# Block 1 of a gated linear-attention kernel: three pair sums on GpSimd, five transposed rows in place of eight on TensorE, and new call orders on all engines

## Chip, cores and metric

The kernel runs on one core of one Trainium2 chip. The metric is the device time of the launch in microseconds (us); for the kernel before it is the median of three runs. Five engines have queues of their own: TensorE (PE), VectorE (DVE), ScalarE (ACT), GpSimd (POOL) and SyncE (SP), which here issues nearly all DMAs. PEld is TensorE's weight load.

## The reference, cut to what matters

The input is 8 sequences of 1024 tokens of width 128. First comes a gated recurrence in 16 heads of size 8, then a feed-forward part of width 512 with three layers between. Both are followed by a residual sum and a normalisation.

```
q, k, v, fg = x@Wq, x@Wk, x@Wv, sigmoid(x@Wf + bf)      # each (b, s, 16, 8)
state = state * fg[..., None] + v[..., None] * k[..., None, :]   # 8x8 per head, step by step
out   = einsum('bhij,bhj->bhi', state, q)
out   = layernorm(out)*gamma + beta;  out = out*silu(x@Wg);  x = layernorm(x + out@Wout)
h = silu(x@w1.T*s1) * (x@w2.T*s2); h = gelu(h@h1.T*..); h = gelu(h@h2.T*..); x = layernorm(x + h@w3.T*..)
```

The sum over j in the einsum is what the change touches: for each block the kernel has eight rows (j = 0 to 7) of Q times state, and they have to be added.

## The kernel before

The 8192 tokens are cut into 16 blocks of 512. Channels lie on the 128 partitions, tokens along the row. `KJ` and `QJ` hold for one block the eight rows of k (then of the state) and of q (then of q times state), 128x512 each, in two buffers that alternate. For blocks 1 to 15 k and q are computed (`project_k`, `project_q`), copied to `qk` by ACT (`copy_k`, `copy_q`), written to memory (`send(n, 1)` for k, `send(n, 0)` for q) and read back spread over the partitions in halves of four rows and 1024 KB (`fetch(n, which, half)`, which = 1 for k).

For a block n the order of the attention part is: `kv` (DVE, two rows each) and `kv_gp` (POOL) multiply k by v; `scan` (DVE, 8 of them) runs the recurrence along the tokens; `qs` (DVE, four, two rows each) multiplies by q; the eight rows are summed; `sum_transposed` (PE) transposes the result into the PSUM bank `back`; `stats_o` (DVE), `rstd_of(n, "o")` (POOL) and `norm_o` (ACT) normalise; `transpose_y`, `affine`, `gated_y` (POOL), `attention_out` (PE), `residual_1`, `stats_1`, `rstd_of(n, "1")`, `norm_1`, `transpose_x1`, `x1_hi` and `x1_lo` follow. The feed-forward part is split into high and low parts of the left operand: `up_hi`/`up_lo(n, t)`, `silu`, `hmul`, then for layers 1 and 2 `mid_open`, `mid_hi`, `mid_lo` with the low parts made by `lo` on POOL, and `last_begin`/`last_rest`. A feed-forward product of 128x512 is one matmul; a projection is two matmul records.

The eight rows are summed in three ways. In block 0 PE adds all eight by transposing into the same bank (`sum_j`). In blocks 2 to 15 DVE adds three times (`add`), POOL once (`add_gp`, line 544), and PE transposes the one row that is left, 4 transposes of 128x128. Block 1 is in `EARLY` (line 27): nobody adds, and PE sums all eight rows by transposes that accumulate, 8 for each of 4 chunks, 32 in all (line 2310). POOL makes four of its k times v rows (`kv_gp(1, 4)` to `(1, 7)`).

Every engine's order is written out by hand as a list of calls; the waits are semaphores inside the helpers. An engine runs its list strictly in order, SP too, so a call that waits holds back all calls behind it. The PSUM bank `front` is shared by all projections other than v, and a table (`FREED`) says which reader each use waits for. `keep_busy` on PE is filler that computes nothing. Everything from block 0's first `up_hi` on is in `rest()`, entered after `set_flag`.

Of the kernel before, what the change touches and what calls it, by code (L numbers as in the profile page):

```python
# [3 lines left out]
def build_program(nc, x_d, xT_d, wproj_d, wffn_d, w3_d, w3s_d, cols_d, ident_d, out_d):  # L4
# [10 lines left out]
    P, T, HD = 128, 512, 8  # L15
# [8 lines left out]
    NPAIR = HD // 2  # L24
    ADDS = 3

    EARLY = range(1, 2)
    XB, XTB, GB = 4, 4, 3
# [9 lines left out]
    with ctx:  # L38
# [86 lines left out]
        def adds_gpsimd(n):  # L125
            return sum(m not in EARLY for m in range(1, n))

# [120 lines left out]
        def _(e):  # L248
# [72 lines left out]
            load_projections(1)  # L321
            load_cols()
            load_xT(1)
            load_weights(0)
            load_weights(1)
            load_weights(2)
            load_xT(2)
            send(1, 1)
# [5 lines left out]
            load_weights(3)  # L334
            send(2, 1)
            load_x(0)
            fetch(1, 0, 0)
# [7 lines left out]
            send(3, 0)  # L345
            load_x(1)
            fetch(2, 0, 1)
            fetch(3, 1, 0)
            send(4, 1)
            fetch(3, 1, 1)  # L350
            load_x(2)
            load_xT(5)
            load_x(3)
            send(4, 0)
            fetch(3, 0, 0)
            load_x(4)
            load_xT(6)
            fetch(3, 0, 1)
            fetch(4, 1, 0)
            fetch(4, 1, 1)  # L360
            fetch(4, 0, 0)
            load_xT(7)
            fetch(4, 0, 1)
            load_xT(8)
            load_x(5)
            send(5, 1)
            fetch(5, 1, 0)
            store(0)
            fetch(5, 1, 1)
            send(5, 0)  # L370
            load_x(6)
            load_xT(9)
            load_x(7)
            store(1)
            fetch(5, 0, 0)
            send(6, 1)
            fetch(5, 0, 1)
            fetch(6, 1, 0)
            send(6, 0)
            fetch(6, 1, 1)  # L380
            store(2)
            fetch(6, 0, 0)
            send(7, 1)
            fetch(6, 0, 1)
            load_xT(10)
            send(7, 0)
            fetch(7, 1, 0)
            fetch(7, 1, 1)
            send(8, 1)
            fetch(7, 0, 0)  # L390
            fetch(7, 0, 1)
            load_x(8)
            store(3)
            fetch(8, 1, 0)
            fetch(8, 1, 1)
            load_x(9)
            send(8, 0)
            send(9, 1)
            fetch(8, 0, 0)
            load_xT(11)  # L400
            fetch(8, 0, 1)
            load_x(10)
            fetch(9, 1, 0)
            send(9, 0)
            load_xT(12)
            fetch(9, 1, 1)
            store(4)
            fetch(9, 0, 0)
# [3 lines left out]
            store(5)  # L412
            send(10, 1)
            fetch(10, 1, 0)
            load_x(11)
            fetch(10, 0, 0)
            fetch(10, 1, 1)
            load_x(12)
            fetch(10, 0, 1)
            send(11, 1)  # L420
            send(11, 0)
            fetch(11, 1, 0)
            fetch(11, 1, 1)
            fetch(11, 0, 0)
            store(6)
            load_x(13)
            send(12, 1)
            fetch(12, 1, 0)
            fetch(11, 0, 1)
            send(12, 0)  # L430
            fetch(12, 1, 1)
            store(7)
            fetch(12, 0, 0)
            load_xT(14)
            send(13, 1)
            fetch(12, 0, 1)
            fetch(13, 1, 0)
            fetch(13, 1, 1)
            load_x(14)
            send(13, 0)  # L440
            store(8)
            load_xT(15)
            fetch(13, 0, 0)
            send(14, 1)
            fetch(14, 1, 0)
            fetch(13, 0, 1)
            store(9)
            fetch(14, 1, 1)
            send(14, 0)
# [4 lines left out]
            fetch(15, 1, 0)  # L454
            fetch(15, 1, 1)
            store(11)
# [3 lines left out]
            load_x(15)  # L460
# [12 lines left out]
        def _(e):  # L473
# [2770 lines left out]
```

## Time and profile before

| quantity | value |
|---|---|
| time, median of 3 runs | 511.95 us (511.7 to 512.26) |
| time of the profiled execution | 511.54 us |
| its span | 509.6 us |
| granted TensorE clock, mean | 0.997 of full |
| PE busy | 496.3 us, 97% |
| DVE busy | 448.7 us, 88% |
| ACT busy | 406.4 us, 80% |
| POOL busy | 311.7 us, 61% |
| DMA traffic | 87.33 MB, mean 171 GB/s |

The busy time of an engine is the union of its records. Matmul records overlap, since their ends are modelled, so the spacing from one group's start to the next is the real cost of matmuls, and a small gap can hide beneath the tail of a record. A row of the timeline merges like instructions: its second number is the stretch covered by all of them. The bracket at a row's end is idle time of that engine ahead of it, with the releaser.

### The profile page before, as it was taken

The numbers are of one execution on the slowest core, as the hardware profiler recorded it, in microseconds if no ns is written. First come the engines' busy times: TensorE is split into PE (matmuls) and PEld (weight loads), VectorE is DVE, ScalarE is ACT, GpSimd is POOL, SyncE is SP. The second block draws the span as 40 slices with busy tenths as digits, with TensorE's granted clock in tenths as the row PEclk, the third lists the DMA queues.
The fourth block names the chain that finished last, engine by engine and source line by source line (L and its number), as shares of the span: only waits on it lengthen the run. The fifth ranks groups of instructions, "written<-read, shape, count | busy, mean of one in ns | idle before, by whom it ended". The sixth has DMA issues, their size and how long they took to land.

```text
span 509.6 us, 7946 instructions
## 1 busy us (share of the span) xinstructions
PE 496.3 (97%) x2528; PEld 382.4 (75%) x2528; DVE 448.7 (88%) x708; ACT 406.4 (80%) x839; POOL 311.7 (61%) x363
## 2 busy tenths in 40 slices
PE   8999999999999999999999999999999999999995
PEld 5576777777878777786877777786877777787995
DVE  4999989999999899998999999899999999993352
ACT  5775968888887888978797788988778987868863
POOL 0751848668392766848385765938477683929432
PEclk9999999999999999999999999999999999999998
DMA  6899999953994497689969675799719483710001
GB/s 244 205 267 236 255 263 241 230 125 84 275 221 104 104 246 177 154 195 249 259 183 234 142 185 125 186 222 244 196 51 235 130 194 94 183 25 1 23 23 44
DMA packets 21500, 87.33 MB, mean 171 GB/s; under 512 B 2512, under 2 KB 3280, under 8 KB 13520
## 3 DMA queue, kind: packets, MB, share of 16 engines
q1 hardware_dynamic: 21168, 86.46, 67.9%
q8 instruction: 22, 0.36, 0.3%
q10 hardware_dynamic: 288, 0.33, 0.2%
q14 instruction: 22, 0.18, 0.1%
HBM read 74.72 MB, written 12.06 MB: 170 GB/s over the span
## 4 chain that ended last, share of the span: by engine, by line
PE 48%; POOL 17%; DVE 13%; issue 13%; ACT 7%; DMA 1%; POOLq 0%; DVEq 0%; ACTq 0%
PE F L2342 26%; POOL h1lo L479 5%; PE front L2243 5%; POOL h2lo L479 5%; PE back L2441 4%; DVE KJ L1590 3%; DVE QJ L1597 2%; POOL KJ L541 2%; DVE QJ L1605 2%; PE ps_v L2243 2%; PE back L2328 2%; PE back L2227 1%; DMA out<-res 1%; POOL rstd_o L511 1%; POOL y L553 1%
## 5 line engine op out<-in xcount | busy, mean ns | idle before, releaser
L903 ACT ACTIVATE h<-F,cols 128x512 f32<-128x512 f32 x120 | 80.7, 686 | 17.0 <-PE F L2342 16.5
L479 POOL TENSOR_TENSOR h1lo<-h,h1hi 128x512 fp32r<-128x512 f32 x60 | 76.5, 1291 | 12.8 <-ACT h1hi L896 12.7
L547 POOL TENSOR_TENSOR QJ<-QJ 128x512 f32<-128x512 f32 x14 | 18.0, 1284 | 108.0 <-DVE QJ L1605 108.0
L479 POOL TENSOR_TENSOR h2lo<-h,h2hi 128x512 fp32r<-128x512 f32 x60 | 77.2, 1309 | 4.9 <-ACT h2hi L896 4.7
L1590 DVE TENSOR_TENSOR_SCAN KJ<-g,carry,KJ 128x512 f32<-128x512 f32 x64 | 78.5, 1263 | 0.9 <-ACT carry L829 0.8
L1590 DVE TENSOR_TENSOR_SCAN KJ<-g,KJ 128x512 f32<-128x512 f32 x64 | 74.3, 1202 | 1.6 <-POOL KJ L528 0.7
L1597 DVE TENSOR_TENSOR QJ<-QJ,KJ 128x1024 f32<-128x1024 f32 x60 | 72.9, 1237 | 0.2
L2342 PE MATMUL F<-h2hi,whi 128*128 128x512 f32 (+1 forms) x256 | 71.6, 415 | 0.8 <-ACT h L903 0.7
L2342 PE MATMUL F<-h1hi,whi 128*128 128x512 f32 (+1 forms) x256 | 68.9, 410 | 1.6 <-DVE h L1654 1.3
L2342 PE MATMUL F<-h1lo,whi 128*128 128x512 f32 (+1 forms) x256 | 67.4, 400 | 0.2 <-POOL h1lo L479 0.2
L2342 PE MATMUL F<-h2lo,whi 128*128 128x512 f32 (+1 forms) x256 | 65.7, 397 | 0.0
L2243 PE MATMUL front<-xT,wproj 128*128 128x512 f32 x122 | 62.9, 597 | 1.4 <-ACT gate L843 0.9
L2342 PEld LDWEIGHTS F<-h1hi,whi 128*128 128x128 f32 x256 | 44.9, 188 | 22.3 <-issue 9.4
L2342 PEld LDWEIGHTS F<-h2hi,whi 128*128 128x128 f32 x256 | 46.6, 188 | 18.6 <-issue 5.7
L2441 PEld LDWEIGHTS back<-w,h 128*128 128x128 f32 x480 | 57.9, 191 | 2.7 <-issue 0.2
L2441 PE MATMUL back<-w,h 128*128 128x128 f32 x480 | 58.4, 275 | 0.0
L2342 PEld LDWEIGHTS F<-h1lo,whi 128*128 128x128 f32 x256 | 45.9, 188 | 12.2 <-issue 2.4
L2342 PEld LDWEIGHTS F<-h2lo,whi 128*128 128x128 f32 x256 | 46.1, 188 | 11.0 <-issue 1.4
L1574 DVE TENSOR_TENSOR KJ<-ps_v,KJ 128x1024 f32<-128x1024 f32 x44 | 52.6, 1206 | 0.0
L1605 DVE TENSOR_TENSOR QJ<-QJ 128x1024 f32<-128x1024 f32 x42 | 51.2, 1220 | 1.4
L890 ACT ACTIVATE h<-F,cols 128x512 f32<-128x512 f32 x60 | 40.3, 685 | 14.7 <-PE F L2342 14.1
L541 POOL TENSOR_TENSOR KJ<-KJ,v_sb 128x512 f32<-128x512 f32 x32 | 41.0, 1288 | 13.0 <-ACT v_sb L864 8.8
(184 smaller groups left out, 935.9 us busy)
## 6 DMA issues: line engine op xcount, KB each, us to landing
KJ<-qk_bounce SPq DMA_DIRECT2D x30, 1024.0 KB, 9.9
QJ<-qk_bounce SPq DMA_DIRECT2D x30, 1024.0 KB, 11.0
qk_bounce<-qk SPq DMA_DIRECT2D x30, 256.0 KB, 4.6
x_in<-in_x SPq DMA_DIRECT2D x16, 256.0 KB, 11.4
xT<-in_xT SPq DMA_DIRECT2D x15, 256.0 KB, 11.5
out<-res SPq DMA_DIRECT2D x15, 256.0 KB, 3.3
wraw<-in_wffn SPq DMA_DIRECT2D x2, 1024.0 KB, 6.6
wraw<-in_wffn SPq DMA_DIRECT2D x2, 256.0 KB, 4.6
```

Source lines behind the costliest of these rows:

```text
L479: e.tensor_tensor(h_lo[layer][:, t, :w], h[:, t, :w], h_hi[layer][:, t, :w].bitcast(f32), ALU.subtract).then_inc(lo_done[layer], 1)
L541: e.tensor_tensor(K, K, v_sb[:, :WIDTH[n]], ALU.mult).then_inc(kv_gp_done, 1)
L547: e.tensor_tensor(first, first, other, ALU.add).then_inc(add_gp_done, 1)
L890: e.activation(h[:, t, :WIDTH[n]], F[2 * (t % 2)][:, :WIDTH[n]], ACT.Silu, scale=S1[t]).then_inc(silu_done, 1)
L903: e.activation(dst[:, t, :WIDTH[n]], F[t][:, :WIDTH[n]], ACT.Gelu, scale=scale[t]).then_inc(gelu_done[layer], 1)
L1574: e.tensor_tensor(K, vb, K, ALU.mult).then_inc(kv_done, 1)
L1590: e.tensor_tensor_scan(K, g[:, :WIDTH[n]], K, init, ALU.mult, ALU.add).then_inc(scan_done, 1)
L1597: e.tensor_tensor(Q, Q, rows(KJ, n)[:, 2 * p:2 * p + 2, :], ALU.mult).then_inc(qs_done, 1)
L1605: e.tensor_tensor(first, first, other, ALU.add).then_inc(add_done, 1)
L2243: return e.matmul(bank[:, :WIDTH[n]], weights, xT[n % XTB][:, :WIDTH[n]], start=True, stop=True)
L2342: return e.matmul(out, whi[:, cs], part, start=start, stop=stop)
L2441: return e.matmul(back[:, chunk(c)], h3[:, k, chunk(c)], w3[:, k, :], start=k == 0, stop=k == NH - 1)
```

## The change

`EARLY_PAIRS = 3` is new. In block 1 POOL now adds rows 0+1, 2+3 and 4+5 of `QJ` in place (`add_pair(1, 0)` to `(1, 2)`), each after the `qs` that makes the pair. PE then transposes rows 0, 2, 4, 6 and 7: 5 for each of 4 chunks, 20 in place of 32. `sum_transposed(1)` waits for the three adds besides the four `qs`.

```diff
+    EARLY_PAIRS = 3
-            return sum(m not in EARLY for m in range(1, n))
+            return sum(EARLY_PAIRS if m in EARLY else 1 for m in range(1, n))
+            def add_pair(n, p):
+                e.wait_ge(qs_done, NPAIR * (n - 1) + p + 1)
+                first, other = (rows(QJ, n)[:, k, :] for k in (2 * p, 2 * p + 1))
+                e.tensor_tensor(first, first, other, ALU.add).then_inc(add_gp_done, 1)
                 if n in EARLY:
                     e.wait_ge(qs_done, NPAIR * n)
-                else:
-                    e.wait_ge(add_gp_done, adds_gpsimd(n + 1))
-                terms = HD if n in EARLY else 1
+                e.wait_ge(add_gp_done, adds_gpsimd(n + 1))
+                terms = [*range(0, 2 * EARLY_PAIRS, 2), *range(2 * EARLY_PAIRS, HD)] if n in EARLY else [0]
```

The rest of the diff, some 2400 lines, reorders calls. No other call is added or dropped on any engine, only their places change, in nearly every block by a few positions. The moves that the prediction speaks of:

```diff
+            load_xT(4)
+            send(3, 1)
+            send(2, 0)
             fetch(2, 1, 0)
-            load_xT(4)
-            send(2, 0)
             fetch(2, 1, 1)
-            send(3, 1)
...
             rstd_of(0, "1")
+            add_pair(1, 0)
             lo(1, 0, 0)
+            add_pair(1, 1)
+            add_pair(1, 2)
             lo(1, 0, 1)
             lo(1, 0, 2)
+            lo(1, 0, 3)
             rstd_of(1, "o")
-            lo(1, 0, 3)
```

- SP (first part of the diff above): the first half of block 2's k is fetched only behind `send(3, 1)` and `send(2, 0)`.
- DVE, old order: `scan(1,6)`, `half_norm("1")`, `qs(1,0)`, `qs(1,1)`, `set_flag`, `x1_lo(0)`, `scan(1,7)`, `qs(1,2)`, `hmul(0,0)`, `hmul(0,1)`, `qs(1,3)`, `hmul(0,2)`, `kv(2,0)`, `hmul(0,3)`, `scan(2,0)`, `stats_o(1)`. New order: `half_norm("1")`, `qs(1,0)`, `set_flag`, `x1_lo(0)`, `qs(1,1)`, `qs(1,2)`, `hmul(0,0)`, `hmul(0,1)`, `scan(1,6)`, `scan(1,7)`, `hmul(0,2)`, `hmul(0,3)`, `qs(1,3)`, `kv(2,0)`, `scan(2,0)`, `stats_o(1)`.
- PE ahead of `rest()`: `project_v(2)` moves from behind `transpose_x1(0)` to behind `sum_j(7)`; `count_low_parts` moves from ahead of `project_k(3)` to behind `transpose_x1(0)`.
- PE in `rest()`, old order: `up_hi(0,0)`, `up_hi(0,1)`, `up_lo(0,0)`, `up_lo(0,1)`, `project_q(3)`, the up products of t = 2 and t = 3, `sum_transposed(1)`, `mid_open(1,0,0..3)`, `mid_hi(1,0,1..3)`, `mid_lo(1,0,0)`. New order: `up_hi(0,0)`, `up_lo(0,0)`, `up_hi(0,1)`, `up_lo(0,1)`, t = 2, `project_q(3)`, t = 3, `project_k(4)`, `mid_open(1,0,0..3)`, `mid_hi(1,0,1)`, `sum_transposed(1)`, `mid_hi(1,0,2..3)`, `mid_lo(1,0,0)`.
- PE, block 4: `up_lo(4,2)` moves from ahead of `up_hi(4,3)` to behind `sum_transposed(5)`, so that `up_lo(4,3)` and `project_gate(6)` alone stand between it and `mid_open(1,4,0)`.
- PE, block 9: `last_rest(8)` moves ahead of `up_hi(9,1)`. Block 14: `project_gate(15)` moves from between `up_lo(14,3)` and `mid_open(1,14,0)` to between `mid_lo(1,13,3)` and `mid_open(2,13,2)`.
- PE, the end: `last_half(0)` moves from behind `tail_lo_products(2,1,3)` to ahead of `tail_lo_products(2,1,0)`, so that `last_half(1)` follows the last low products at once.

## Rows read from the trace of the kernel before

**Rows 1.** The page: busy us, share and instructions; granted clock; DMA share, 40 slices.

```profile
PE 496.3 (97%) x2528; PEld 382.4 (75%) x2528; DVE 448.7 (88%) x708; ACT 406.4 (80%) x839; POOL 311.7 (61%) x363
...
PEclk9999999999999999999999999999999999999998
DMA  6899999953994497689969675799719483710001
```

**Rows 2.** The page: shares by engine of the chain that ended last.

```profile
PE 48%; POOL 17%; DVE 13%; issue 13%; ACT 7%; DMA 1%; POOLq 0%; DVEq 0%; ACTq 0%
```

**Rows 3.** Timeline of PE, 41 to 53 us: start, length, work [idle before <-releaser].

```profile
41.44 0.60 PE L2227 MATMUL back<-ident,x 128*128 128x128 f32 x4
41.88 1.02 PE L2243 MATMUL ps_v<-xT,wproj 128*128 128x512 f32 x2
42.74 1.02 PE L2243 MATMUL front<-xT,wproj 128*128 128x512 f32 x2
43.99 1.19 PE L2342 MATMUL F<-x1hi,whi 128*128 128x512 f32 x4 [0.23 <-issue]
...
47.21 0.73 PE L2342 MATMUL F<-x1hi,whi 128*128 128x512 f32 x2 [0.24 <-DVE h L1654]
...
49.17 3.65 PE L2310 MATMUL back<-ident,QJ 128*128 128x128 f32 x32
52.58 3.98 PE L2342 MATMUL F<-h1hi,whi 128*128 128x512 f32 x16
```

**Rows 4.** Timeline of DVE, 42 to 73 us.

```profile
42.77 0.68 DVE L1649 TENSOR_TENSOR x1lo<-back,x1hi 128x512 fp32r<-128x512 f32 x1
...
49.83 1.21 DVE L1574 TENSOR_TENSOR KJ<-ps_v,KJ 128x1024 f32<-128x1024 f32 x1
...
51.79 1.22 DVE L1590 TENSOR_TENSOR_SCAN KJ<-g,KJ 128x512 f32<-128x512 f32 x1
...
72.90 0.69 DVE L1649 TENSOR_TENSOR x1lo<-back,x1hi 128x512 fp32r<-128x512 f32 x1 [2.24 <-ACT x1hi L883]
```

**Rows 5.** Timeline of POOL, 49 to 57 us.

```profile
49.73 3.78 POOL L479 TENSOR_TENSOR h1lo<-h,h1hi 128x512 fp32r<-128x512 f32 x3 [10.38 <-ACT h1hi L896]
...
55.83 1.31 POOL L479 TENSOR_TENSOR h1lo<-h,h1hi 128x512 fp32r<-128x512 f32 x1
```

**Rows 6.** Timeline of ACT, then of SP, around 44 and 34 us.

```profile
43.80 0.60 ACT L819 ACTIVATE qk<-front 128x512 f32<-128x512 f32 x1 [1.07 <-PE front L2243]
...
33.71 0.51 SPq L294 DMA_DIRECT2D KJ<-qk_bounce  x1
```

**Rows 7.** KJ's fetches, us from issue to landing: at 33.71; all 30; at 13.8.

```profile
DMA to landing us min/median/max: 15.3/15.3/15.3
...
DMA to landing us min/median/max: 7.7/9.9/21.9
...
KJ<-qk_bounce SPq DMA_DIRECT2D x1, 1024.0 KB, 12.4
```

**Rows 8.** Timeline of PE at four later waits.

```profile
71.39 0.66 PE L2227 MATMUL back<-ident,x 128*128 128x128 f32 x4 [0.45 <-ACT x L848]
...
314.71 0.63 PE L2310 MATMUL back<-ident,QJ 128*128 128x128 f32 x4 [0.42 <-DVE res L1662]
...
443.62 2.59 PE L2342 MATMUL F<-h2hi,whi 128*128 128x512 f32 x10 [0.39 <-ACT h L903]
...
460.55 3.15 PE L2342 MATMUL F<-h1hi,whi 128*128 128x512 f32 x12 [0.24 <-DVE h L1654]
```

**Rows 9.** Timeline of the end: PE's last products, and ACT's last gelu.

```profile
500.55 3.73 PE L2472 MATMUL F<-w,h 128*128 128x128 f32 x32
...
501.01 0.51 ACT L916 ACTIVATE h<-back,cols 128x256 f32<-128x256 f32 x1
```

**Rows 10.** Instructions by line: min/median/max ns of one, first and last start.

```profile
L1597 DVE TENSOR_TENSOR QJ<-QJ,KJ x60: 1193/1214/1779, 40.4 to 452.4; 128x1024 f32<-128x1024 f32 x60
...
L479 POOL TENSOR_TENSOR h2lo<-h,h2hi x60: 1263/1296/2285, 61.5 to 473.0; 128x512 fp32r<-128x512 f32 x60
```

More of the change, by code:

```diff
@@ L391, in _ @@
             fetch(7, 0, 1)
+            fetch(8, 1, 0)
+            send(8, 0)
+            fetch(8, 1, 1)
+            store(3)
+            load_x(7)
+            fetch(8, 0, 0)
+            fetch(8, 0, 1)
+            load_xT(11)
+            send(9, 1)
+            load_xT(12)
+            fetch(9, 1, 0)
             load_x(8)
-            store(3)
-            fetch(8, 1, 0)
-            fetch(8, 1, 1)
+            send(9, 0)
+            store(4)
+            fetch(9, 1, 1)
+            send(10, 1)
             load_x(9)
[L397 to L401, printed above, removed]
-            load_x(10)
[L403 to L408, printed above, removed]
+            fetch(9, 0, 0)
+            load_x(10)
+            store(5)
             load_xT(13)
@@ L1776, in _ @@
             hmul(0, 1)
+            scan(1, 6)
+            scan(1, 7)
+            hmul(0, 2)
+            hmul(0, 3)
             qs(1, 3)
-            hmul(0, 2)
             kv(2, 0)
-            hmul(0, 3)
             scan(2, 0)
@@ L1861, in _ @@
             hmul(3, 3)
+            stats_o(4)
             scan(5, 0)
-            stats_o(4)
             kv(5, 1)
+            scan(5, 1)
             kv(5, 2)
-            scan(5, 1)
             scan(5, 2)
@@ L2010, in _ @@
             scan(10, 7)
+            x1_lo(9)
             qs(10, 1)
@@ L2013, in _ @@
             add(10, 0)
-            x1_lo(9)
             qs(10, 3)
@@ L2484, in rest @@
                 up_hi(0, 0, low_parts)
+                up_lo(0, 0, low_parts)
                 up_hi(0, 1, low_parts)
-                up_lo(0, 0, low_parts)
                 up_lo(0, 1, low_parts)
-                project_q(3)
                 up_hi(0, 2, low_parts)
                 up_lo(0, 2, low_parts)
+                project_q(3)
                 up_hi(0, 3, low_parts)
                 up_lo(0, 3, low_parts)
-                sum_transposed(1)
+                project_k(4)
                 mid_open(1, 0, 0, low_parts)
@@ L2671, in rest @@
                 mid_lo(1, 4, 3, low_parts)
+                project_q(7)
                 mid_open(2, 4, 2, low_parts)
-                project_q(7)
-                project_v(7)
-                project_gate(7)
                 mid_open(2, 4, 3, low_parts)
@@ L2684, in rest @@
                 mid_lo(2, 4, 3, low_parts)
+                up_hi(5, 0, low_parts)
                 last_begin(4)
-                up_hi(5, 0, low_parts)
+                last_rest(4)
                 up_lo(5, 0, low_parts)
-                last_rest(4)
                 up_hi(5, 1, low_parts)
+                project_gate(7)
                 up_lo(5, 1, low_parts)
-                project_k(8)
-                sum_transposed(6)
                 up_hi(5, 2, low_parts)
                 up_lo(5, 2, low_parts)
+                sum_transposed(6)
+                project_k(8)
                 up_hi(5, 3, low_parts)
@@ L2801, in rest @@
                 mid_lo(2, 7, 0, low_parts)
+                project_v(10)
+                project_k(11)
                 mid_lo(2, 7, 1, low_parts)
+                transpose_x1(8)
                 mid_lo(2, 7, 2, low_parts)
[L2804 to L2805 removed]
                 mid_lo(2, 7, 3, low_parts)
[L2807 removed]
                 up_hi(8, 0, low_parts)
+                up_lo(8, 0, low_parts)
                 last_begin(7)
[L2810 removed]
+                last_rest(7)
                 up_hi(8, 1, low_parts)
[L2812 removed]
                 up_lo(8, 1, low_parts)
+                project_gate(10)
                 up_hi(8, 2, low_parts)
[L2815 removed]
                 sum_transposed(9)
@@ L3173, in _ @@
             sum_j(3)
-            project_q(1)
-            project_qj(7)
             sum_j(4)
             sum_j(5)
+            project_qj(7)
+            project_f(2)
             sum_j(6)
             sum_j(7)
-            project_f(2)
+            project_v(2)
+            project_gate(1)
             keep_busy(4, back)
             keep_busy(1, back)
-            project_gate(1)
             project_f(3)
```

976 lines of the change are left out of this document (483 added, 493 removed).

## Prediction, made before the changed kernel was run

> **What bounds the kernel now.** I read the page from the top. PE is busy 97% of the span at full clock in all but the last slice, DVE 88%, POOL 61% [rows 1]. The chain that ended last runs through PE for 48% and goes through POOL and DVE for 30% [rows 2]. So nothing waits long, but PE is held up by small waits that come from the other engines, and it is PE's queue whose length sets the end. The DMA share is 0.9 or more from the third to the eighth slice, 25 to 102 us [rows 1], so early on the memory traffic is a resource as well. A change therefore pays by what it takes from PE's queue and by the PE waits it adds or removes. The idle time of POOL, 10.38 us ahead of its first `lo` [rows 5], costs nothing and can hold work.
>
> The sum is made against the profiled execution, 511.54 us (span 509.6 and 1.9 around it). The median of the three runs is 511.95, 0.41 above, and the answer is carried to the median.
>
> **A. The transposes.** The 32 transposes of block 1 start at 49.17 and the next PE group at 52.58 [rows 3]: 3.41 us, or 0.107 each. The records are 0.27 long but overlap, so the spacing counts. Twelve go: 12 x 0.107 = 1.28 us off PE's queue. Nothing covers them, PE is the engine that is full. **-1.28**, bounds 0 (a wait takes their place) and -1.28.
>
> **The adds.** Three POOL operations of 128x512. POOL's other operations of that shape take 1.29 to 1.31 [rows 5, 10], so 3 x 1.29 = 3.9 us. The first lies in the 10.38 us of idle time. The other two stand behind `lo(1,0,0)` and ahead of the three `lo` that `mid_lo(1,0,0)` needs. Before, the last `lo` ran 55.83 to 57.14 and PE reached `mid_lo` at about 56.4 (52.58 plus 3.8 for 16 products) [rows 3, 5]: no slack. Now `rstd_of(1, "o")` goes behind the `lo`s, `hi(1,0,0)` comes before the third `silu`, and PE starts the round earlier (B), so I expect the first `lo` near 46.6. Adds to 50.5 at the latest, three `lo` to 54.4; PE needs them near 55. I cost it at **0**; if the first `lo` stays at 49.73, the last ends at 49.73 + 6 x 1.26 = 57.3, and PE waits 2.4.
>
> What would the adds do to DVE? One of the 60 `qs` took 1.779 against a median of 1.214, and one POOL `lo` 2.285 against 1.296 [rows 10]: if these are places where the two met, a meeting puts 0.57 on DVE or 0.99 on POOL. I expect one such meeting, hidden behind DVE's 2.24 us of idle time at 72.90 [rows 4]. The Trainium skill, "SBUF — State Buffer", section on the shared port, speaks against this change: a VectorE tensor_tensor with two SBUF inputs and a GpSimd operation that reads SBUF exclude each other for a whole instruction. By that rule the adds belong where DVE reads no two SBUF operands; the two long records agree that it happens, though not how often.
>
> **B. Earlier start of `rest()`.** Between the x1 transposes and the first up product PE does `project_v(2)`, 41.88 to 42.74, then `project_q(2)`, and starts at 43.99 [rows 3]. `project_v(2)` (0.86) moves to where PE runs filler and waits for DVE anyway. `x1_lo(0)` ran at 42.77 behind a scan and two `qs` [rows 4]; with one scan and one `qs` fewer ahead of it, it is ready in time. `count_low_parts` changes sides but PE does it in either case. **-0.86**, bounds 0 (the flag comes late) and -1.25 (all of the 41.88 to 43.99 but `project_q(2)`).
>
> **C. New waits in block 0's round.** The third up pair waits for silu and `hmul` of the first. Before, `project_q(3)` (0.86) stood between and PE was still idle 0.24 [rows 3]. Now the cover is gone, but `up_lo(0,0)` comes 0.47 earlier: +0.4. The 3.41 us of transposes that covered the last `hmul`s are gone from there, `project_k(4)` (0.86) stands instead, and two scans of 1.2 lie ahead of `hmul(0,2)`: I take +0.4 more. **+0.8**, bounds 0 and 2.5.
>
> **D. Block 14.** `project_gate(15)` covered 0.86 of the wait for `hmul(14,2)`, after which PE was still idle 0.24 [rows 8]. That cover is gone: +0.86. At its new place it covers a gelu wait, 0.39 in the record and about 0.45 in spacing [rows 8]. **+0.4**, bounds -0.4 and +0.9.
>
> **E. The end.** `last_half(1)` now stands right behind the last low products. The last gelu ended at 501.52, about 0.97 after the start of PE's final group at 500.55 [rows 9]; three of the four products of its first chunk fill 0.66 of this. **+0.3**, bounds 0 and 0.9. `last_half(0)`'s earlier finish gives nothing, since the chain behind the second half ends last.
>
> **F. The rest of the reordering.** Two waits should go: 0.45 at block 1's x1 transposes (`rstd_of(1, "1")` now passes a `lo`) and 0.42 at block 10's sum, which waited for a residual (`last_rest(8)` is earlier) [rows 8]. In block 4 a cover shrinks by 0.86, +0.4. Elsewhere calls move by one to three places, and about as often away from their producer as towards it; I found neither side ahead. **-0.47**, bounds -2 and +2, since PE's gaps over blocks 1 to 14 make that scale (509.6 less 496.3 is 13.3 us with start and end).
>
> **The SP queue.** `fetch(2,1,0)` was issued at 33.71 and took 15.3 us to land, at 49.0 [rows 6, 7]; `kv(2,0)` used it at 49.83 [rows 4]. Now it is queued behind `send(3,1)` and `send(2,0)`, and the latter waits for `copy_q(2)`, which ended at 44.4 before [rows 6] and should at about 43.5 now. Landing takes 7.7 at the least and 9.9 in the median [rows 7]: 51.2 to 53.4. DVE, which must also do qs and two scans first, reaches `kv(2,0)` at about 51. With 7.7 nothing is lost, since `stats_o(1)` waits for PE until 53.7; I take this, because the earlier fetches are then through. Behind the waiting `kv(2,0)` stand `scan(2,0)` and `stats_o(1)`, and behind those POOL's `rstd_of(1,"o")` and PE's `transpose_y(1)`. Cost **0**, up to 4.9 if it takes 12.4 as the second fetch of block 1's pair did [rows 7].
>
> **Sum.** -1.28 - 0.86 + 0.8 + 0.4 + 0.3 - 0.47 = -1.11. 511.54 - 1.11 = 510.43 for the profiled execution, 510.84 as a median, say **510.9**.
>
> **Rivals.**
>
> 1. *Everything is covered.* C, D and E cost nothing: -1.28 - 0.86 - 0.47 = -2.6, 509.3. For it: most waits at PE are 0.2 to 0.4 now. Against it: the covers that were taken away are named above, and two of them left a wait even while they were there. Chance 0.18.
> 2. *The gain is eaten.* C at 1.9 in place of 0.8, because the `hmul`s behind two scans come late: 0.0, 511.9. Chance 0.12.
> 3. *Slower: block 2's k lands late.* The place is `kv(2,0)`. With a landing 12.4 after 43.5, at 55.9, DVE stands 4.9 us; its idle time of 2.24 at 72.90 takes up part [rows 4], the other 2.7 reaches PE through `transpose_y(1)` and `sum_transposed(2)`: -1.1 + 2.7 = +1.6, 513.5. It decides from a landing at about 53.2 on. For it: the DMA engines are full there [rows 1], and this very fetch took 15.3 before. Against it: it then stood behind 2 MB of earlier fetches. Two other ways give nearly the same time and are counted here: the late `lo` above (-1.1 + 2.4 = +1.3, 513.2), and adds that each hold DVE for a whole operation (3.9 less the 2.24 covered, -1.1 + 1.7 = +0.6, 512.5). Chance 0.25.
>
> That the edit does nothing is ruled out, the transposes are plainly fewer.
>
> **How the numbers follow.** Likeliest case (sum above, own range 509.9 to 511.8): 0.45. A measurement of this kernel can tell about 0.2%, 1.0 us, from no change. The likeliest case lies across that bound: 0.27 faster, 0.17 within, 0.01 slower. Rival 1 is faster, rival 2 within, rival 3 slower by 0.23 and within by 0.02. Together faster 0.45, same 0.31, slower 0.24. The range takes in rival 1 and most of rival 3: 508.9 to 513.8.
>
> **What would show it.** A right: 20 records of block 1's sum, in about 2.1 us. B: first up product at about 43.1. Adds: the first in POOL's old idle time, no PE wait ahead of the first `h1lo` product. C: PE idle at the third up pair and at the first `h1hi` product, 0.8 together. SP: `fetch(2,1,0)` issued near 43.5 and `kv(2,0)` without idle time ahead of it; an idle DVE of over 2 us there means rival 3. D: a wait of about 1.1 at block 14's first `h1hi` product. E: a gap of 0.3 in PE's last 16 products. The prediction is wrong if PE's waits between blocks 2 and 13, which I netted at nearly nothing, change by more than 2 us in sum.

## The result, and the profile after

The changed kernel takes 515.85 us (median of 6 runs, 514.7 to 516.82), beside 512.05 us for the kernel before on the same chip (511.7 to 512.82): a ratio of 1.0071, 95% interval 1.0059 to 1.0084. The forecast was 510.9, faster; the change is slower by 3.8 us. The profiled execution took 515.69 us with a span of 513.8 us.

The page after, in the parts of [rows 1, 2]: busy us and instructions of each engine, granted clock, DMA share, and the chain that ended last by engine.

```profile
PE 497.5 (97%) x2516; PEld 381.5 (74%) x2516; DVE 448.8 (87%) x708; ACT 406.4 (79%) x839; POOL 314.1 (61%) x366
...
PEclk9999999999999999999999999999999999999999
DMA  6996999973597874998983479648748971700001
...
PE 48%; POOL 21%; issue 16%; ACT 7%; DVE 7%; POOLq 0%; DVEq 0%; ACTq 0%
```

PE has 12 instructions fewer and the same 97%, in a span that is 4.2 us longer. POOL and "issue" have a larger part of the chain than before (21% and 16% against 17% and 13%), DVE a smaller one (7% against 13%), so these shares alone don't tell where the time went. Around block 0's round, timeline of PE (the stretch of [rows 3]):

```profile
43.08 0.34 PE L2488 MATMUL F<-ones_col,low_any 128*1 128x1 f32 x8
43.35 1.12 PE L2252 MATMUL front<-xT,wproj 128*128 128x512 f32 x2
45.04 0.72 PE L2350 MATMUL F<-x1hi,whi 128*128 128x512 f32 x2 [0.56 <-issue]
...
47.79 0.73 PE L2350 MATMUL F<-x1hi,whi 128*128 128x512 f32 x2 [0.65 <-DVE h L1663]
...
51.95 2.23 PE L2350 MATMUL F<-h1hi,whi 128*128 128x512 f32 x8 [0.29 <-DVE h L1663]
54.02 2.35 PE L2318 MATMUL back<-ident,QJ 128*128 128x128 f32 x20
56.12 2.10 PE L2350 MATMUL F<-h1hi,whi 128*128 128x512 f32 x8
...
61.42 0.63 PE L2236 MATMUL back<-ident,o_norm 128*128 128x128 f32 x4 [0.40 <-ACT o_norm L857]
```

The same stretch on DVE (beside [rows 4]), on POOL (beside [rows 5]) and on SP (beside [rows 6]):

```profile
43.46 0.15 DVE L1733 CAST flag<-F 1x1 int32<-1x1 f32 x1 [0.76 <-PE F L2488]
...
53.61 1.23 DVE L1583 TENSOR_TENSOR KJ<-ps_v,KJ 128x1024 f32<-128x1024 f32 x1
```

```profile
42.78 1.27 POOL L553 TENSOR_TENSOR QJ<-QJ 128x512 f32<-128x512 f32 x1 [1.85 <-DVE QJ L1606]
48.61 1.27 POOL L480 TENSOR_TENSOR h1lo<-h,h1hi 128x512 fp32r<-128x512 f32 x1 [4.57 <-ACT h1hi L905]
49.84 2.52 POOL L553 TENSOR_TENSOR QJ<-QJ 128x512 f32<-128x512 f32 x2
52.89 4.35 POOL L480 TENSOR_TENSOR h1lo<-h,h1hi 128x512 fp32r<-128x512 f32 x3 [0.54 <-ACT h1hi L905]
```

```profile
45.64 1.18 SPq L295 DMA_DIRECT2D KJ<-qk_bounce  x2
```

The 20 transposes take 54.02 to 56.12, 2.10 us, as forecast. And block 0 is only one of many places. To see the others, I take for each block the distance between its first up product and the next block's, and subtract what PE's work between them costs, each piece at its spacing in the trace (0.233 for a product of 128x512, 0.86 for a projection, 2.13 or 3.41 for block 1's transposes, and so on). What is left is stall, in us; its level is right to some tenths a block, while its differences between runs are better, since the same prices are used for all.

```
block          0    1    2    3    4    5    6    7    8    9   10   11   12   13   14    sum
before       1.61 0.89 1.06 0.07 1.25 0.77 1.05 0.07 1.07 0.79 1.42 0.90 0.66 1.86 1.84  15.31
after        2.57 1.19 0.66 0.72 0.95 2.46 0.50 1.26 0.91 1.21 0.97 0.85 0.76 1.11 2.62  18.74
```

Blocks 0 to 8 lost 3.38 (7.84 before, 11.22 after); blocks 9 to 14 together lost nothing (7.47 and 7.52). The account of the two profiled executions, whose spans differ by 4.2: first up product at 45.04 in place of 43.99, +1.05; work -1.28; stall +3.43; from the first product of the last block to the last residual (478.04 to 504.32, and 481.24 to 507.82) 26.58 in place of 26.28, +0.30; the rest, nearly all of it the landing of the last store, +0.70. The sum is 4.2. Where the profile names the stalls of the later blocks, PE's timeline after has these rows (the sum of block 6, which falls in block 5's round, the first `h1hi` product of blocks 13 and 14, and the end; the last two stand beside [rows 8, 9]):

```profile
198.37 0.66 PE L2318 MATMUL back<-ident,QJ 128*128 128x128 f32 x4 [0.97 <-POOL QJ L548]
...
436.48 3.16 PE L2350 MATMUL F<-h1hi,whi 128*128 128x512 f32 x12 [0.62 <-DVE h L1663]
...
463.75 2.47 PE L2350 MATMUL F<-h1hi,whi 128*128 128x512 f32 x9 [1.20 <-DVE h L1663]
...
505.67 2.11 PE L2480 MATMUL F<-w,h 128*128 128x128 f32 x16
```

### The profile page after: what moved, and what is told of

It is laid out like the page before. It is cut to its first block, busy times and chain, and to the rows that moved or that the text cites. A ratio compares the mean times of both kernels' runs of the same rounds, so it can differ in the third digit from the quotient of the medians.

```text
span 513.8 us, 7925 instructions
## 1 busy us (share of the span) xinstructions
PE 497.5 (97%) x2516; PEld 381.5 (74%) x2516; DVE 448.8 (87%) x708; ACT 406.4 (79%) x839; POOL 314.1 (61%) x366
## 4 chain that ended last, share of the span: by engine, by line
PE 48%; POOL 21%; issue 16%; ACT 7%; DVE 7%; POOLq 0%; DVEq 0%; ACTq 0%
PE F L2350 27%; POOL h1lo L480 5%; POOL h2lo L480 5%; PE back L2449 5%; PE front L2252 5%; POOL KJ L542 3%; DVE KJ L1599 2%; PE back L2236 2%; POOL rstd_o L512 2%; PE back L2336 1%; PE ps_v L2252 1%; POOL rstd L498 1%; POOL y L559 1%; PE F L2248 1%; POOL QJ L548 1%
## 5 line engine op out<-in xcount | busy, mean ns | idle before, releaser
L480 POOL TENSOR_TENSOR h2lo<-h,h2hi 128x512 fp32r<-128x512 f32 x60 | 76.1, 1289 | 12.4 <-ACT h2hi L905 12.4
L2350 PE MATMUL F<-h1hi,whi 128*128 128x512 f32 (+1 forms) x256 | 71.4, 416 | 3.3 <-DVE h L1663 3.2
L1606 DVE TENSOR_TENSOR QJ<-QJ,KJ 128x1024 f32<-128x1024 f32 x60 | 71.2, 1213 | 0.4 <-DMA QJ<-qk_bounce 0.3
```

The source lines that it names most:

```text
L480: e.tensor_tensor(h_lo[layer][:, t, :w], h[:, t, :w], h_hi[layer][:, t, :w].bitcast(f32), ALU.subtract).then_inc(lo_done[layer], 1)
L1606: e.tensor_tensor(Q, Q, rows(KJ, n)[:, 2 * p:2 * p + 2, :], ALU.mult).then_inc(qs_done, 1)
L2350: return e.matmul(out, whi[:, cs], part, start=start, stop=stop)
```

## The experiments

Each was timed beside the kernel before. "Ratio" is to that, with its 95% interval; stall and starts are of its profiled execution.

| run | us | ratio | first up product | stall, blocks 0 to 14 |
|---|---|---|---|---|
| 1 pairs alone, old orders | 512.24 | 1.0007 (0.9998 to 1.0016) | 43.77 | 16.49 |
| 2 new orders, no pairs | 516.38 | 1.0093 (1.0078 to 1.0109) | 44.89 | 17.95 |
| 3 old start | 515.21 | 1.0065 (1.0052 to 1.0079) | 43.34 | 18.41 |
| 4 old SyncE order | 541.84 | 1.0576 (1.0558 to 1.0594) | 44.78 | 46.53 |
| 5 run 1, center_w3 early | 512.42 | 1.0003 (0.9989 to 1.0017) | 44.71 | 16.46 |
| 6 run 5, rstd_of(1, "1") early | 512.08 | 0.9997 (0.9987 to 1.0006) | 43.90 | 16.22 |
| 7 old end | 515.22 | 1.0059 (1.0041 to 1.0076) | 43.69 | 19.02 |
| 8 add_gp(6) first | 515.2 | 1.0058 (1.004 to 1.0077) | 44.39 | 19.10 |
| 9 run 6, stats_o(1) early | 511.56 | 0.9983 (0.9972 to 0.9993) | 45.11 | 15.26 |
| 10 project_gate(15) back | 515.96 | 1.0077 (1.0064 to 1.009) | 44.02 | 19.85 |
| 11 run 8, store(6) later | 521.18 | 1.0156 (1.0127 to 1.0186) | 43.56 | 25.56 |
| 12 project_v(10) back | 520.17 | 1.0145 (1.013 to 1.016) | 45.03 | 24.86 |
| 13 run 9 without pairs | 512.33 | 1.0000 (0.9991 to 1.0009) | 45.05 | 14.79 |
| 14 new orders until block 8 | 513.72 | 1.0034 (1.0023 to 1.0046) | 44.59 | 18.01 |
| 15 old orders until block 8 | 515.43 | 1.0071 (1.0055 to 1.0087) | 43.97 | 19.24 |
| 16 run 9, lo(1, 0, 3) first | 513.19 | 1.0019 (1.0004 to 1.0033) | 44.58 | 18.17 |

### The pairs by themselves (runs 1, 5, 6, 9, 13, 16)

Run 1: the kernel before, with this.

```diff
             rstd_of(0, "1")
+            add_pair(1, 0)
+            add_pair(1, 1)
+            add_pair(1, 2)
             lo(1, 0, 0)
```

> The kernel before with the three pair adds and the 20 transposes alone; every other call where it was, the three adds on GpSimd in a row ahead of the first lo, in the idle time of 10.38 us. Theory (the pairs pay, the new orders cost): 12 transposes fewer, 1.28 us faster less a wait of up to 0.8 at the last low part of block 0's first middle layer, so 510.8 to 511.6, PE's first product of that layer at 51.3 in place of 52.58. Rival (the adds themselves cost, by holding VectorE or by making low parts late): no faster than before, 512.0 or more, and VectorE operations of over 1.5 us between 41 and 50 us.

512.24 us, ratio 1.0007: no gain, the number of the rival. Timeline of PE, then of ACT and DVE:

```profile
48.95 2.34 PE L2318 MATMUL back<-ident,QJ 128*128 128x128 f32 x20
51.05 3.08 PE L2350 MATMUL F<-h1hi,whi 128*128 128x512 f32 x12
55.09 1.19 PE L2350 MATMUL F<-h1hi,whi 128*128 128x512 f32 x4 [0.96 <-ACT h1hi L905]
```

```profile
54.43 0.61 ACT L905 ACTIVATE h1hi<-h 128x512 fp32r<-128x512 f32 x1
...
44.33 1.68 DVE L1606 TENSOR_TENSOR QJ<-QJ,KJ 128x1024 f32<-128x1024 f32 x1
```

Counted from its first up product (43.77, before 43.99), PE is 1.3 ahead after the transposes (51.05, before 52.58) and stops 0.96 for the fourth `h1hi`, which stands on ACT behind `center_w3`. From block 0's first up product to block 1's it is 30.37, to the hundredth what it was before. The rival's sign is there too, but small: one `qs` took 1.68 and two adds 3.43 in place of 2.5, and DVE still had 0.17 idle before its next operation. The two adds one by one, on POOL, and the `qs` under way at the first, on DVE:

```profile
41.49 2.18 POOL L553 TENSOR_TENSOR QJ<-QJ 128x512 f32<-128x512 f32 x1 [2.38 <-DVE QJ L1606]
43.64 1.28 POOL L553 TENSOR_TENSOR QJ<-QJ 128x512 f32<-128x512 f32 x1
...
41.33 1.22 DVE L1606 TENSOR_TENSOR QJ<-QJ,KJ 128x1024 f32<-128x1024 f32 x1
```

The Trainium skill, "SBUF — State Buffer", section "Who interferes with whom", has them exclude each other: the one that begins second waits until the first is through. This trace agrees. The add that began at 41.49, behind the `qs` of 41.33, ended 1.1 after it; the `qs` of 44.33, begun during the add of 43.64, ended 1.1 after that. By itself such an operation takes 1.2 to 1.3. The other two `qs` met no add.

Run 5 moves `center_w3` to the start of ACT's list.

> The kernel before with the pair adds (as in the first experiment) and one call moved on ScalarE: center_w3, 2.5 us of work on the last layer's weights, goes from behind g_of_tanh(2) in block 0's round to behind copy_v(1) at the start. Theory (the 1.28 us of the transposes is eaten because ScalarE is late: the fourth h1hi at 54.43 stands behind center_w3, PE waits 0.96 for it, and then block 1's attention chain through VectorE, which the transposes don't shorten): the wait of 0.96 goes, but the wait of 0.45 ahead of block 1's x1 transposes grows by as much, so the first up product of block 1 stays within 0.4 of 30.37 after block 0's, and the total stays at 511.5 to 512.2. Rival (ScalarE's wait was all that stood in the way): 1.0 us faster than with the pairs alone, 511.2, block 0's period 29.4.

512.42, nothing gained, as the theory had it, but at another place than it said: the wait at block 1's x1 transposes stayed (0.48). PE's wait for `h1hi` went and this one came, in the same round:

```profile
57.87 0.50 PE L2350 MATMUL F<-h1lo,whi 128*128 128x512 f32 x1 [1.16 <-POOL h1lo L480]
```

Run 6 adds, on GpSimd, `rstd_of(1, "1")` ahead of `lo(2, 0, 3)`.

> As the run above, and on GpSimd rstd_of(1, "1") moved ahead of lo(2, 0, 3), as in the changed kernel. Theory (two locks in a row, ScalarE's order and then block 1's norm): the wait ahead of the x1 transposes of block 1 is gone, and only now the 1.28 us shows, block 0's period 29.2 to 29.6 in place of 30.37, total 510.8 to 511.2. Rival (the period is bound further back, by VectorE's kv, scan and stats_o of block 1, whose start the transposes don't move): the period stays at 30.0 or more and the total at 511.5 to 512.2.

512.08, the rival: no time was gained. The wait at block 1's x1 transposes was gone, the wait for `h1lo` stayed at 1.18, the period was 30.14. The `lo` stood behind `rstd_of(1, "o")`, and that behind DVE's `stats_o(1)` at 52.84, though the last of the 20 transposes ended 1.4 us earlier. So run 9:

```diff
             hmul(0, 3)
+            stats_o(1)
             scan(2, 0)
-            stats_o(1)
```

> The sixth run's kernel (old orders, pair adds, center_w3 at the start, rstd_of(1, "1") ahead of a lo) with one more call moved: on VectorE stats_o(1) ahead of scan(2, 0). PE there waited 1.18 for the last lo of block 0's first layer, which stood on GpSimd behind rstd_of(1, "o"), and that behind stats_o(1) at 52.84, 1.6 us after the last of the 20 transposes. Theory (this was the next lock: VectorE's order kept the earlier sum from being used): stats_o(1) 1.2 earlier, PE's wait of 1.18 gone, block 0's period 29.1 in place of 30.14, total 511.0. Rival (yet another lock, the fetch for which VectorE waits 0.47 at kv(2, 1), or a later block takes the gain back): period 29.6 or more, or total 511.8 or more.

511.56, ratio 0.9983 (0.9972 to 0.9993): faster than the kernel before, and the only kernel here that is, by 1.0 of 512.57. Block 0's period fell to 29.30 (theory 29.1), its stall from 2.66 to 1.82, and PE's wait for the `lo` to 0.37:

```profile
57.48 0.50 PE L2350 MATMUL F<-h1lo,whi 128*128 128x512 f32 x1 [0.37 <-POOL h1lo L480]
```

Run 13 takes the pairs out again and keeps the three moved calls.

> The ninth run's kernel without the pair sums: 32 transposes again, and center_w3, rstd_of(1, "1") and stats_o(1) where the ninth had them. Theory (the pairs give the gain, the moves only let it through): 511.56 + 1.0 = 512.5, block 0's period back at 30.2. Rival (the moves are the gain, the transposes are still covered): 511.6 to 511.9.

512.33, ratio 1.0000, as the theory had it: 0.77 above run 9 by the medians, 0.9 by the two ratios. From first up product to the last block it is 433.53 against 432.72. So the pair sums are worth about 0.8 us once one call on each of three other engines has made way, and nothing before. Run 16 swaps the last `lo` with `rstd_of(1, "o")`.

> The ninth run's kernel with lo(1, 0, 3) ahead of rstd_of(1, "o") on GpSimd. PE still waited 0.37 for that lo. Theory (last of the locks in block 0): 0.3 us faster than the ninth, 511.2, as o_norm, 1.3 later, is still in time for transpose_y(1), which stands behind one more product group. Rival (o_norm is what is late then, and the chain to the x1 transposes of block 1 by 1.3): 512.0 or more.

513.19: the rival, and by more than it said. `o_norm` came late for `transpose_y(1)`, and block 0's stall rose to 4.73:

```profile
58.69 0.63 PE L2236 MATMUL back<-ident,o_norm 128*128 128x128 f32 x4 [1.88 <-ACT o_norm L857]
```

### Pairs or orders (run 2)

The changed kernel with `EARLY_PAIRS = 0` and no `add_pair`.

> The changed kernel without the pair adds: 32 transposes again, all new orders kept. Theory (pairs worth 1.28 in either order): 515.85 + 1.3 = 517.1. Rival (the adds are what costs in the new orders, where two of them stand between the first and the second lo): 515.85 or less. Where the changed kernel lost 4 us after block 1 it still must lose it.

516.38, between the theory and the rival: 0.5 above the changed kernel by the medians, 1.1 by the ratios, and the two intervals overlap. In the traces block 0's period was 31.37 against 30.05: here the new orders let the whole 1.28 through. But block 5's stall was 1.91 against 2.46 and block 9's 0.95 against 1.21, so at the last block only 0.5 was left (436.69 against 436.20). These two stalls differ as much between executions of the same lists (block 5: 1.98 in run 7; block 9: 1.52 there), so how much of the 1.28 reaches the end in the new orders is open. What costs is the orders: against the same orders before, they are 3.6 us slower with pairs (runs of after and 1) and 4.4 without (run 2 and before).

### The start (runs 3 and, for comparison, all others)

> The changed kernel with the old orders of all engines up to the flag (projections and sums of block 0, the loads of the start, ScalarE up to copy_q(2), VectorE up to scan(1,5)); the new orders from there on. Theory (the start of the changed kernel is really 1.05 us later, by its order): first up product back at about 44.0 to 44.4 and the whole 0.7 to 1.0 faster, 514.9 to 515.2. Rival (the late start was TensorE's clock, which came up at 7.4 us in place of 4.8 in that execution, and has nothing to do with the order): same total as the changed kernel, 515.8, and the changed kernel's own runs differ by a microsecond between each other.

515.21, 0.6 less and within the spread of the changed kernel. The first up product came at 43.34, 1.70 earlier, and the stall sum was nearly the same (18.41). The key is in the weight loads (PEld) of the first projections, first of before, then of after:

```profile
5.38 0.19 PEld L2243 LDWEIGHTS F<-xT,wproj 128*128 128x128 f32 x1 [0.24 <-issue]
5.81 0.19 PEld L2243 LDWEIGHTS F<-xT,wproj 128*128 128x128 f32 x1 [0.24 <-issue]
```

```profile
5.88 0.34 PEld L2252 LDWEIGHTS ps_v<-xT,wproj 128*128 128x128 f32 x1 [0.52 <-issue]
6.74 0.34 PEld L2252 LDWEIGHTS ps_v<-xT,wproj 128*128 128x128 f32 x1 [0.52 <-issue]
7.49 0.19 PEld L2252 LDWEIGHTS F<-xT,wproj 128*128 128x128 f32 x1 [0.41 <-issue]
```

A load takes 0.34 and a product's spacing is 0.86, then 0.19 and 0.43. I read this as TensorE at the lower of its two levels (1.2 and 2.4 GHz) and then at the higher, since the spacing halves. After the same 16 warm-up products from 1.45 us on, the short loads began by 4.9 us in seven of the eighteen profiled executions (before, runs 1, 3, 6, 7, 11 and 15), between 5.5 and 6.5 in seven more (runs 2, 5, 8, 10, 13, 14 and 16), and at 7.3 to 7.6 in four (after, runs 4, 9 and 12). The same lists are found early and late: run 7 had the rise by 4.4 and its first up product at 43.69, the changed kernel at 7.5 and 45.04. With the early rise the old start gave 43.77 to 43.99 and the new one 43.56 and 43.69 (runs 11, 7); with the late one 45.11 (run 9) and 44.78 to 45.04 (after, runs 4 and 12); in between the two overlap (44.58 to 45.05 and 44.02 to 44.89). So the +1.05 of the comparison is the moment at which the clock rose in one execution, and the new start is worth some 0.1 to 0.3. Run 3, with the early rise, was earlier than either: it has `project_v(2)` and `count_low_parts` at their old places on PE, but DVE's new calls around the flag, which ran at 40.97, and PE went from `project_q(2)` to the first up product without a bracket. That suggests that the calls on DVE helped and PE's two moves took it back; neither was run alone. The Trainium skill, "TensorE: Matmul & The Clock Gate", section on the HAM clock gate, says that the moment varies from run to run, since the hardware's observation does not begin with the kernel, and puts that at half a microsecond either way. The traces agree that it varies, but by about 3 us from first to last; they don't show the reason.

### The end (run 7)

> The changed kernel with the old orders of all engines after the last products of block 14's second layer. Theory (the new order of the end costs what the traces show, 32.56 against 31.56 from the first tail product to the end): 1.0 us faster than the changed kernel, 514.9, with 0.3 of it in PE's stream and 0.7 between PE's last product and the end. Rival (the end only inherits a delay from before): no difference, 515.8.

515.22. The part on PE, from the first product of the last block to the last residual, was 26.27 to 26.29 with the old end (nine profiled executions, of before and of runs 1, 5, 6, 7, 9, 13, 14 and 16) and 26.57 to 26.59 with the new one (the other nine): 0.30, nearly to the hundredth. From the last normalisation to the end of the span, where only the last stores land, it was 2.21 to 2.69 with the old end (mean 2.45) and 2.51 to 3.00 with the new (mean 2.83). So of the 0.70 in the comparison about 0.4 goes with the order, by a cause that I did not look for, and the rest is spread. The theory took a part of the difference between two single executions for an effect of the order. The medians, 0.6 apart, fit the 0.7 that is left, but the two ratios' intervals overlap.

### The losses between blocks 1 and 14 (runs 8, 11, 12, 10, 4)

Run 8 moves `add_gp(6)` ahead of `kv_gp(7, 6)` on GpSimd. POOL, after and then run 8:

```profile
195.79 1.30 POOL L542 TENSOR_TENSOR KJ<-KJ,v_sb 128x512 f32<-128x512 f32 x1 [9.74 <-DMA KJ<-qk_bounce]
197.04 1.28 POOL L548 TENSOR_TENSOR QJ<-QJ 128x512 f32<-128x512 f32 x1
```

```profile
193.28 1.30 POOL L548 TENSOR_TENSOR QJ<-QJ 128x512 f32<-128x512 f32 x1 [7.93 <-DVE QJ L1614]
194.53 2.54 POOL L542 TENSOR_TENSOR KJ<-KJ,v_sb 128x512 f32<-128x512 f32 x2
```

> The changed kernel with one call moved: GpSimd's add_gp(6) ahead of kv_gp(7, 6), which waits 9.74 us for a fetch. Theory (that one place costs up to 0.97, PE's wait for the sum of block 6): PE's wait there is gone and the period of block 5 falls from 30.17 to 29.6 or less; total 0.5 to 0.9 faster, 515.0 to 515.3. Rival (the wait is covered by a later one): the period falls but a later block takes it back, total 515.8.

Block 5's stall fell from 2.46 to 1.13 (1.91 and 1.98 in runs 3 and 7, with the lists of after there), as the theory had it: 0.8 to 1.3 of it came from the order of these two calls. Whether the kernel gained is open. The median, 515.2, is the theory's, but the intervals of its ratio and of the changed kernel's overlap for the most part; in the trace blocks 8 and 9 rose from 0.91 and 1.21 to 1.49 and 2.16, as the rival says, and from the first up product to the last block it is 436.56 against 436.20. But those two blocks had 2.87 in sum in run 7 and 3.25 in run 10 too, whose lists there are those of after, so their rise can't be put down to the swap. The place is the second half of block 11's k, which the kernels with the new SyncE order issue at 305.5 to 307.3 behind `store(6)` (before: 295.75), so that it lands when it is already due. From run 8, PE and POOL:

```profile
300.18 1.13 PE L2252 MATMUL ps_v<-xT,wproj 128*128 128x512 f32 x2 [0.44 <-DVE KJ L1583]
...
314.81 1.29 POOL L542 TENSOR_TENSOR KJ<-KJ,v_sb 128x512 f32<-128x512 f32 x1 [1.14 <-DMA KJ<-qk_bounce]
```

It took 7.5 us to land in run 3 (block 9's stall 0.99), 7.7 in after (1.21), 8.0 in run 7 (1.52), 8.5 in run 10 (2.02) and 8.7 in run 8 (2.16). Run 11 therefore puts the fetches first.

```diff
             fetch(11, 1, 0)
-            store(6)
             fetch(11, 1, 1)
             fetch(11, 0, 0)
             fetch(11, 0, 1)
+            store(6)
```

> The changed kernel with add_gp(6) first, as in the eighth run, and on SyncE store(6) moved behind the three fetches of block 11 that stood behind it. There fetch(11, 1, 1) was issued at 306 to 307 us, behind a store that waits for a norm, and landed 7.5 to 8.7 us later, when GpSimd and VectorE were already due; in the kernel before it was issued at 295. Theory (block 9's stall of 0.95 to 2.16 follows the landing of this fetch, and it takes back what the swap gives in block 5): block 9's stall falls to 0.8 or less, and the 1.3 of block 5 stays, total 1.5 to 2 us faster than the changed kernel, 514.0. Rival (VectorE or the norms are what is late in block 9): the stall stays at 1.5 or more, total 515.2.

521.18 (five of its six runs between 520.8 and 521.6, one at 516.42). Both were wrong. Of the four fetches, issued between 289.53 and 295.89, the first was just landing when the store was issued at 304.41. The store took 14.1 us: it landed at 318.5, 0.3 after the last of them. In after, issued at 306.95 ahead of three fetches, it had taken 2.0. DVE's `residual_2(8)` needs that buffer, PE's sum of block 10 needs the bank that the residual reads:

```profile
318.62 0.69 DVE L1671 TENSOR_TENSOR res<-back,x 128x512 f32<-128x512 f32 x1 [5.76 <-DMA out<-res]
...
319.45 1.09 PE L2318 MATMUL back<-ident,QJ 128*128 128x128 f32 x4 [5.45 <-DVE res L1671]
```

Run 12 puts `project_v(10)` back between `mid_lo(2, 7, 3)` and `up_hi(8, 0)`, in PE's list alone.

> The changed kernel with project_v(10) back between mid_lo(2, 7, 3) and up_hi(8, 0), where it covers a wait for a gelu. Block 7's stall in the changed kernel is 1.26 against 0.07. Theory (it is a cover that went, 0.43 of the 1.19): block 7's stall falls by 0.4, total 0.4 faster, 515.4. Rival (v of block 10 comes later by it, and VectorE's kv(10, ...) with it): block 8 or 9 loses what block 7 gains.

520.17, and neither: block 7's stall was 4.38 in place of 1.26 and block 8's 3.72 in place of 0.91. ACT's new list has `copy_v(10)` ahead of `x1_hi(8)` and the last gelus, and it now waited for PE, which then waited for them (ACT, then PE, in block 7; block 8 I did not follow):

```profile
281.48 0.60 ACT L873 ACTIVATE v_sb<-ps_v 128x512 f32<-128x512 f32 x1 [2.98 <-PE ps_v L2252]
...
283.88 1.12 PE L2350 MATMUL F<-x1hi,whi 128*128 128x512 f32 x2 [2.43 <-ACT h L912]
```

Run 10 puts `project_gate(15)` back, PE's list alone as well.

> The changed kernel with project_gate(15) back between up_lo(14, 3) and mid_open(1, 14, 0). Theory (step D of the prediction: a projection is a cover of 0.86, and the wait of 1.20 ahead of block 14's first h1hi product is the cover that went): block 14 gains 0.85, block 13 loses 0.4 at a gelu wait, together 0.4 faster, 515.4. Rival (what it covers in block 13 is worth as much): no change, 515.8.

515.96, the rival. Block 14's stall fell from 2.62 to 1.81 and block 13's rose from 1.11 to 1.94: nothing either way. Run 4 puts SyncE's old list under the new ones.

> The changed kernel with SyncE's old order of loads, sends, fetches and stores; all other orders new. Theory (the waits are in the orders of the computing engines): within 0.5 us of 515.85, with GpSimd's wait of 9.7 us for a fetch of block 7's k gone, and 0.5 to 1 us gained at the sum of block 6's rows. Rival (the DMA order is the main cause): 513 or less.

541.84, both wrong by far. Blocks 5 and 14 took 40.47 and 40.83 in place of 30.17 and 26.96, and block 0 another 4.0; in block 5 POOL waited 18.61 for a fetch and PE 9.77 for POOL's add:

```profile
208.38 1.26 POOL L542 TENSOR_TENSOR KJ<-KJ,v_sb 128x512 f32<-128x512 f32 x1 [18.61 <-DMA KJ<-qk_bounce]
...
210.92 1.11 PE L2318 MATMUL back<-ident,QJ 128*128 128x128 f32 x4 [9.77 <-POOL QJ L548]
```

The lists of the five engines are one schedule; one of the old with four of the new is worse than either.

### Does the loss add up (runs 14, 15)

All engines change lists at about block 8's second layer.

> The changed kernel's orders on all engines up to about block 8's second layer (SyncE up to send(10, 0)), and the old orders from there on, with the pair sums. Theory (the losses add up by place: stalls of blocks 0 to 8 as in the changed kernel, 11.2 against 7.8, blocks 9 to 14 and the end as before): blocks 9 to 14 at 7.5 in place of 7.5 to 8.5, the end 1.0 less, so 514.3. Rival (one coupled chain: what is late is made up or lost again in the other half): 512.5 or less, or 515.8.

513.72: blocks 0 to 8 had 10.83 of stall (after 11.22, before 7.84), blocks 9 to 14 7.18 (before 7.47), the end 26.29. The theory, with 0.6 less than it said. The late first half did not make the second half later.

> The old orders up to the same point, with the pair sums in a row, and the new orders from there on. Theory (adding up): blocks 0 to 8 as with the pairs alone (9.1), the rest as in the changed kernel with 1.0 for the end and 0 to 1 for blocks 9 to 14: 513.2 to 514.2. Rival (the new second half is only slow because the first half feeds it late): 512.2, as with the pairs alone.

515.43, 1.2 to 2.2 more than the theory said, and 3.2 more than the rival: block 8, where the lists are joined, had 3.18 in place of 1.05, and block 9 had 1.74. The other blocks had the stall of their own list (0 to 7: 8.05, beside 8.04 in run 1; 10 to 14: 6.27, beside 6.31 in the changed kernel; PE's end 26.58). So the loss of the changed kernel belongs to its places: nearly all of PE's is in blocks 0 to 8 and 0.3 is at the end. The total of run 15 is mostly its seam and says less than run 14.

## Why the prediction was wrong, point by point

- **A, the transposes, -1.28.** The price is right: 20 in 2.10 us. That nothing covered them was wrong as it stood. "PE is the engine that is full" was read from 97% busy [rows 1], but in run 1 each tenth that PE won was lost again within the round, at ACT's, then POOL's, then DVE's place in their lists. In the new orders block 0 let it through (31.37 to 30.05); how much of it reached the end is not settled (run 2). Best case here: 0.8 (runs 9, 13).
- **The adds, 0.** Right in the total, with other times: the first `lo` at 48.61 (forecast 46.6), the last three from 52.89 in 4.35, the first of them 1.86 long because a `qs` had begun at 52.38, and no PE wait for them. The adds themselves met no `qs` in the changed kernel; they did in run 1.
- **B, -0.86.** Wrong. The flag became what was late: `count_low_parts`, now behind the x1 transposes, ran at 43.08, `set_flag` at 43.46 with 0.76 idle before it, and the first up product followed only 1.6 later. That was inside the bounds as "the flag comes late"; I had waved it aside because "PE does it in either case". At equal clock the start gained some 0.1 to 0.3. Run 3, with `project_v(2)` and `count_low_parts` left at their old places, gained 0.4 to 0.6 over the old start.
- **C, +0.8.** Right: 0.65 at the third up pair and 0.29 at the first `h1hi`; block 0's stall rose by 0.96.
- **D, +0.4.** The wait of about 1.1 is there (1.20), but the gain at the new place is 0.8 and not 0.45: 0 in sum (run 10).
- **E, +0.3.** Right: 0.30.
- **SP.** `fetch(2, 1, 0)` was issued at 45.64, 2.1 later than forecast, and landed at 53.59, 0.4 behind the bound at which rival 3 decides. `kv(2, 0)` at 53.61 had no idle time before it all the same, since DVE came there only then. So rival 3 did not happen, by luck in part: in run 3, where DVE was earlier, it did wait 0.81 there.
- **F, -0.47, is the step that failed.** Both waits that should go went: no bracket at block 1's x1 transposes or at block 10's sum. But over blocks 1 to 14 the stall rose by 2.47, and D is nothing in that, so F measured about +2.5 where I had -0.47 and bounds of -2 to +2. The largest pieces are block 5 (+1.69), block 7 (+1.19) and block 3 (+0.65), against -0.55 and -0.40 in blocks 6 and 2; block 4, where I had +0.4 for a smaller cover, came out at -0.30. I had counted moves "towards and away from the producer" and found them balanced. But one single move can outweigh many: `kv_gp(7, 6)`, which waits for a DMA, now stands before `add_gp(6)`, which PE needs, and putting it back took 0.8 to 1.3 off block 5 (run 8). `fetch(11, 1, 1)` behind `store(6)` is of the same kind, and block 9's stall follows its landing; here the run that was to show it (11) failed, so that is argued. Both can be read in the diff. My own mark for this, PE's waits between blocks 2 and 13 off by more than 2 us in sum, was set too wide: they are off by 1.39 in these traces, and by 2.47 with blocks 1 and 14.

Sum of the steps as measured, in the profiled executions: -1.28 (A), about -0.2 (B), +0.96 (C), 0 (D), +0.30 (E), +2.5 (F), which is +2.3; the other 1.9 of the 4.2 are the clock's rise (about 1.2, at equal starts) and the last store (0.7). The medians differ by 3.8. Of the last two only the 0.4 of the store goes with the order, which makes 2.7; blocks 8 and 9 had 2.12 of stall in the profiled execution of after but 2.87 and 3.25 in runs 7 and 10, whose lists are the same there, so the landing of block 11's fetch adds some tenths that a single trace doesn't show. About 1 us of the 3.8 is not assigned. The causes of the stalls in blocks 3 and 7 are open. For block 7 the profile of after has two brackets where that of before has none, both for ACT:

```profile
261.38 1.12 PE L2252 MATMUL front<-xT,wproj 128*128 128x512 f32 x2 [0.23 <-ACT qk L828]
...
280.93 0.73 PE L2350 MATMUL F<-x1hi,whi 128*128 128x512 f32 x2 [0.20 <-ACT h L912]
```

One suspected cover was tried there in PE's list alone (run 12), and that only broke the match with ACT's list. So the failed step is known, and that the new orders cause it is shown (runs 1, 2 and 14); of its single causes one is shown, block 5's.

## What to carry to other kernels

In a schedule where the computing engines' strict queues are 61 to 97% full, taking work from the fullest one pays only as far as the others' lists let its next inputs come earlier: follow each input that the shortened stretch waits for next to the call that stands in front of its producer, and move that too (here one call on each of three engines for 0.8 us). In a long reordering don't net moves by count. Look for the calls that wait for a DMA, see what now stands behind each of them on its queue, and give every such place its own term. To put back a part of one engine's list alone is a gamble, since each was fitted to the other four: one projection cost 4 us that way (run 12), another nothing (run 10), and SyncE's whole list 26 (run 4).

## What the runs showed of the hardware

- TensorE's change to short weight loads, read here as its rise to the higher level, came by 4.9 us in some executions, at about 7.5 in others and in between in the rest, behind the same warm-up products. Between the early and the late ones the first up product moved by 1.1 to 1.5 us. The granted clock shows nothing of it, it is 1.00 there in both; only the durations of the weight loads (0.34 and 0.19) and the spacing of the products (0.86 and 0.43) do. Windows of after, 4.8 to 6 and 6 to 7.4 us, granted clock third from the end:

```profile
4.80:6.00 1.20, 1.20 (x5) 0.68 (x4) 0.59 (x1) 0.20 (x1) 0.00 (x0) 1.00 0.96 325
6.00:7.40 1.40, 1.40 (x3) 0.56 (x2) 0.10 (x1) 0.36 (x1) 0.00 (x0) 1.00 1.10 414
```

- A store of 256 KB landed in 2.0 us when three fetches of 1024 KB were issued behind it (after), and in 14.1 when three such fetches, issued 8.5 us and more before it, had still to land (run 11). In run 11 all five landed in the order of issue.
- A DVE operation with both inputs in SBUF (`qs`, or an add) and a POOL operation of 128x512 don't run side by side. In the traces of before, after and run 1 there are 28 such pairs whose records overlap by more than 0.06 us, and in each the one that began second ended 1.08 to 1.18 us after the first had ended, little less than the 1.2 to 1.3 us that it takes alone.
